# First stage of a fused attention kernel: both gate blocks side by side in eight PSUM banks, first loads one tile at a time

## The chip, the cores and the metric

One Trainium2 chip, one of its cores. The metric is the device time of one execution in microseconds, median of several runs. The kernel before took 1560.95 us (three runs, 1560.48 to 1561.99).

## What is computed

Four batches, 1024 rows of x (1024 wide) and 2048 rows of memory (512 wide) each:

```
memory_proj    = memory @ W_mem.T                    # W_mem is 1024 x 512
scores         = x @ memory_proj.T / sqrt(1024)
attn           = softmax(scores)
memory_context = attn @ memory_proj
gate           = sigmoid([x, memory_context] @ W_gate.T + b_gate) # W_gate is 1024 x 2048
out            = rmsnorm(x + gate * memory_context) * norm_w
```

The left half of W_gate (columns 0 to 1023) is applied to x, its right half to the memory context. The kernel doesn't form memory_proj. It multiplies x by W_mem first (q, 512 wide) and attends over the raw memory; and it multiplies the right half of W_gate by W_mem once (`wc`, 512 by 1024), to be applied to the attended raw memory at the end.

## The kernel before

All matmuls are 128x512 in fp32r. Every operand is held as a high part (an fp32r copy that ScalarE makes) and a low part (the difference, which VectorE makes, line 311), and every product is three matmuls (`PASSES`: high-high, high-low, low-high), 128 rows of depth at a time.

The program runs through stages. The first (up to the last matmul of line 1604 before line 1645) computes ten blocks of 512 columns: G0 and G1, the two halves of W_gate's right half, whose products with W_mem are `wc`; then X0 to X7, the 4096 rows of x, whose products are q. A block is 8 tiles of depth (t) by 4 tiles of columns of W_mem (c) by 3 passes: 96 matmuls. A block's four results stand in PSUM banks 0 to 3. ScalarE copies them out (`evacuate`), and they go to DRAM (`store_wc`, `store_q`). The later stages are the gate's part on x, the attention over 32 units of 128 rows, and the gate's part on the context with the norm.

On the way to a block each engine has a part of the work:

- SyncE issues all loads and stores of the stage, in one fixed order, and each waits for what it needs. The first loads come in three groups (`LEAD`: tiles 0-1, 2-3, 4-7), each first of W_mem and then of G0, four DMAs for each, one for each 32 partitions. After them come half blocks ("G1a", "X0b"; `load_half`, 1 MB each as four DMAs) into the two halves of the buffer `a_in`, in the order of the table `HALVES`. That table also holds "E0a" to "E1b", the left half of W_gate, which the next stage needs.
- VectorE transposes in blocks of 32 by 32: G0 tile by tile (128x512, line 259), all else by halves (128x2048, line 991), from `a_in` to `a_tf`. Then it makes the low parts.
- ScalarE makes the high parts, of W_mem (line 707), of G0's tiles (line 732) and of halves (line 711), and copies the banks out (lines 719 and 721).
- TensorE runs G0 tile by tile (`block_q0`), then nine blocks in a loop (`block_q`). A block needs its half (`xt_ready`) and its banks back (`q_ready`).

The transposed operand has one place, `a_xt`, 16 tiles in high and low. Half a of the next block may be split into it only when TensorE has passed the first half of the block before (`q_half`), and half b when it has finished that block (`q_done`). The results go out over the one buffer `prob`.

Of the kernel before, what the change touches and what calls it, by code (L numbers as in the profile page):

```python
# [20 lines left out]
def build(nc, x, mem, w_mem, w_gate, b_gate, norm_w, out):  # L21
# [28 lines left out]
    with ExitStack() as ctx:  # L50
# [37 lines left out]
        a_wc = prob[:].rearrange("p (c n) -> p c n", c=CT)  # L88
# [91 lines left out]
        def unit_tile(tile, u):  # L180
# [14 lines left out]
        w_loaded, g0_loaded = [sem(f"w_loaded{h}") for h in range(3)], [sem(f"g0_loaded{h}") for h in range(3)]  # L195
        w_hi, w_ready, g0_tile_t = sem("w_hi"), sem("w_ready"), sem("g0_tile_t")
        x0_tile_hi, x0_tile_ready = sem("x0_tile_hi"), sem("x0_tile_ready")
# [39 lines left out]
        HALVES = ("G1a", "G1b", "X0a", "X0b", "E0a", "X1a", "X1b", "E0b", "X2a", "X2b", "E1a", "X3a", "X3b", "E1b",  # L237
                  "X4a", "X4b", "X5a", "X5b", "X6a", "X6b", "X7a", "X7b")
# [23 lines left out]
        def tile_count(own, halves, t):  # L262

            return (halves, t // HT + 1) if t % HT == HT - 1 else (own, t - t // HT + 1)

        def tile_of_tf(t):
            return a_tf[:, BANK * t:BANK * (t + 1)]


        LEAD = ((0, 2), (2, 4), (4, 8))  # L270

        def lead_of(t):

            return t // 2 if t < HT else 2

        def w_piece(lead, n):

            lo, hi = LEAD[lead]
            src = a_wf.rearrange("p t (q c j) -> p t c q j", q=NQ, j=SQ)
            if lead == 2:  # L280
                ts, c = slice(lo, hi), n
                return (src[:, ts, c], *(a_w[:, part, ts, P * c:P * (c + 1)].rearrange("p t (q j) -> p t q j", q=NQ)
                                         for part in (HI, LO)))
            t, cs = lo + n // 2, range(2 * (n % 2), 2 * (n % 2) + 2)
            return (src[:, t, cs[0]:cs[1] + 1],
                    *(a_w[:, part, t, P * cs[0]:P * (cs[1] + 1)].rearrange("p (c q j) -> p c q j", q=NQ, j=SQ)
                      for part in (HI, LO)))

        def w_count(t, c):

            return 2 * t + c // 2 + 1 if t < HT else 2 * HT + c + 1
# [48 lines left out]
        def _(sp):  # L340
            for h, (lo, hi) in enumerate(LEAD):
                for q in range(NQ):
                    sp.dma_start(a_wf[SQ * q:SQ * (q + 1), lo:hi],
                                 w_mem[CHX * q + SQ * lo:CHX * q + SQ * hi, :].rearrange(
                                     "(t j) c -> j t c", j=SQ)).then_inc(w_loaded[h], 16)
                load_quadrants(sp, a_in, w_gate[0:BANK, D:2 * D], D, g0_loaded[h],
                               part=(lo // (hi - lo), DT // (hi - lo)))

            def load_half(name):
                n, k, h = nth(name) - 1, int(name[1]), "ab".index(name[2])  # L350
                if n < 2:
                    sp.wait_ge(g0_tile_t, HT * (n + 1))
# [4 lines left out]
                else:  # L357
                    src = w_gate[BANK * k:BANK * (k + 1), D * "EG".index(name[0]):D * "EG".index(name[0]) + D]
# [11 lines left out]
            def store_wc(k):  # L370
                sp.wait_ge(q_ready, CT * (k + 1))
                sp.dma_start(wc_dram[:, :, BANK * k:BANK * (k + 1)], a_wc).then_inc(block_stored, 16)
# [11 lines left out]
            load_half("X1b")  # L384
            load_half("E0b")
            store_wc(1)
            load_half("X2a")
            store_raw(1)
            load_half("X2b")
            load_half("E1a")  # L390
            store_q(0)
            load_half("X3a")
            load_half("X3b")
            load_half("E1b")
            store_q(1)
            load_half("X4a")
            load_half("X4b")
# [304 lines left out]
        def _(act):  # L702
            def split_w(lead):
                act.wait_ge(w_loaded[lead], 16 * NQ)
                for n in range(CT):
                    src, hi, _ = w_piece(lead, n)
                    nc.scalar.copy(hi, src).then_inc(w_hi, 1)  # L707

# [5 lines left out]
            def evacuate(k, c):  # L714
                if c == 0 and k > 0:
                    act.wait_ge(block_stored, 16 * k)
                act.wait_ge(q_done, k * CT + c + 1)
                if k < GB:
                    nc.scalar.copy(a_wc[:, c], bank[c][:]).then_inc(q_ready, 1)
# [7 lines left out]
            for t in range(DT):  # L727
                if t == LEAD[lead_of(t)][0]:
                    split_w(lead_of(t))
                act.wait_ge(g0_tile_t, t + 1)  # L730
                signal, _ = tile_count(x0_tile_hi, xt_hi, t)
                nc.scalar.copy(a_xt[:, HI, t, :], tile_of_tf(t)).then_inc(signal, 1)
            for k in range(LAST):
                following = BLOCKS[k + 1]
                act.wait_ge(half_t, nth(following + "a"))
                act.wait_ge(q_half, k + 1)
# [5 lines left out]
                if following == "X0":  # L742
                    act.wait_ge(half_t, nth("E0a"))
                    w7_split(A11, ef_x)
                if following == "X1":
                    act.wait_ge(half_t, nth("E0b"))
                    w7_split(A12, ef_y)
                if following == "X3":
# [21 lines left out]
            act.wait_ge(q_half, NBLOCKS)  # L770
# [210 lines left out]
        def _(dve):  # L981
            def split_w(lead):
                for n in range(CT):
                    dve.wait_ge(w_hi, lead * CT + n + 1)
                    src, hi, lo = w_piece(lead, n)
                    minus_hi(lo, src, hi).then_inc(w_ready, 1)

# [43 lines left out]

            for lead in range(len(LEAD)):
                split_w(lead)
                dve.wait_ge(g0_loaded[lead], 16 * NQ)
# [801 lines left out]
```

## Time and profile before

| | us |
|---|---|
| median of three runs | 1560.95 |
| the profiled execution's own time | 1556.9 |
| its span in the trace | 1555.1 |
| TensorE busy | 1528.3 (98%) |
| VectorE busy | 1080.3 (69%) |
| ScalarE busy | 549.0 (35%) |
| first matmul starts | 9.94 |
| last matmul of the first stage ends (first of line 1645 starts) | 231.60 |

The span is from the first to the last instruction. The profiled execution's own time is 1.8 us more than its span, and 4.05 us below the median of the runs without a profile. Start times below are counted from the start of the span. The record of a matmul runs until its modelled end, so that matmuls overlap: their starts say more than their busy time. A few matmul records are missing from the trace, so counts in a stretch are slightly low.

### The profile page before, as it was taken

Reading aid. Unit: us, or ns where it says so; the run is one execution under the profiler, and the core shown is the slowest. Engines: PE = TensorE matmul, PEld = TensorE weight load, DVE = VectorE, ACT = ScalarE, POOL = GpSimd, SP = SyncE. Lnnn points to the kernel's source line nnn. Section 1 sums busy time; section 2 is a strip of 40 time slices with the busy share of each in tenths; the row PEclk is TensorE's granted clock in tenths of the full one; section 3 lists DMA queues with packets and bytes.
Section 4 is the critical chain, followed back from the end, with each engine's and each line's share of the span. In section 5 each row is a group of like instructions: output and inputs, shape, how many; then the busy total and the mean of one; then the engine's idle time right before and its main releaser. Section 6 shows DMA issues by size and latency. Waiting matters only on the chain.

```text
span 1555.1 us, 21137 instructions
## 1 busy us (share of the span) xinstructions
PE 1528.3 (98%) x6720; PEld 1262.0 (81%) x6720; DVE 1080.3 (69%) x1502; ACT 549.0 (35%) x919; POOL 33.3 (2%) x72
## 2 busy tenths in 40 slices
PE   7999999999999999999999999999999999999997
PEld 5888888888888878888788888888888888888886
DVE  5654758777777864467446754567555899989987
ACT  4232342222222352244222432234222554444443
POOL 0000000000000000000000000000000001100011
PEclk9999999999999999999999999999999999999999
DMA  9997526333332786757584666757748645555553
GB/s 197 235 241 178 127 88 175 113 113 113 108 108 95 171 214 158 180 142 189 154 208 131 166 166 172 181 139 196 189 133 282 215 181 191 194 197 197 198 198 120
DMA packets 213399, 262.63 MB, mean 169 GB/s; under 512 B 19312, under 2 KB 136048, under 8 KB 213104
## 3 DMA queue, kind: packets, MB, share of 16 engines
q1 hardware_dynamic: 213360, 262.20, 59.8%
q8 instruction: 13, 0.21, 0.1%
q14 instruction: 26, 0.21, 0.1%
HBM read 170.39 MB, written 89.65 MB: 167 GB/s over the span
## 4 chain that ended last, share of the span: by engine, by line
PE 44%; DMA 3%; DVE 1%; issue 1%; ACT 1%; SPq 1%; POOL 0%; ACTq 0%; DVEq 0%; POOLq 0%
PE bank L1604 25%; PE bank L1753 19%; DMA prob_scratch<-prob 2%; DMA region_f<-in_ctx 1%; DMA region_f<-prob_scratch 1%; ACT prob L807 1%; DVE region_l L311 0%; SPq L453 0%; DVE region_n L311 0%; DVE max_part L1232 0%; DVE region_f L1328 0%; SPq L509 0%; ACT region_t L818 0%; ACT region_l L825 0%; POOL mean_sq L693 0%
## 5 line engine op out<-in xcount | busy, mean ns | idle before, releaser
L1604 PE MATMUL bank<-region_n,region_l 128*128 128x512 f32 x1536 | 353.6, 389 | 2.6 <-DVE region_l L311 2.6
L1604 PE MATMUL bank<-region_t,region_l 128*128 128x512 f32 x1536 | 353.7, 389 | 2.2 <-DVE region_l L311 2.1
L1604 PEld LDWEIGHTS bank<-region_t,region_l 128*128 128x128 f32 x1536 | 288.0, 188 | 63.8 <-issue 4.2
L1604 PEld LDWEIGHTS bank<-region_n,region_l 128*128 128x128 f32 x1536 | 288.2, 188 | 63.1 <-DVE region_l L311 2.9
L1604 PE MATMUL bank<-region_t,region_n 128*128 128x512 f32 x960 | 220.2, 392 | 11.6 <-DVE region_t L311 11.6
L1604 PEld LDWEIGHTS bank<-region_t,region_n 128*128 128x128 f32 x960 | 181.4, 189 | 49.9 <-DVE region_t L311 12.0
L825 ACT CAST region_l<-bank 128x512 fp32r<-128x512 f32 x128 | 75.0, 586 | 329.2 <-DVE bank L1261 329.0
L1261 DVE STREAM_TRANSPOSE bank<-region_f 128x512 f32<-128x512 f32 x128 | 88.7, 716 | 102.5 <-DMA region_f<-prob_scratch 100.3
L311 DVE TENSOR_TENSOR region_t<-region_f,region_t 128x1024 fp32r<-128x1024 f32 (+2 forms) x77 | 110.5, 1466 | 67.3 <-ACT region_t L711 60.5
L1645 PE MATMUL bank<-region_t,region_l 128*128 128x512 f32 x576 | 135.7, 389 | 0.0
L1645 PEld LDWEIGHTS bank<-region_t,region_l 128*128 128x128 f32 x576 | 108.1, 188 | 22.4
L1753 PE MATMUL bank<-region_t,region_l 128*128 128x512 f32 x480 | 120.6, 389 | 0.2 <-DVE region_l L311 0.2
L1753 PE MATMUL bank<-region_n,region_l 128*128 128x512 f32 x480 | 120.5, 389 | 0.0
L807 ACT ACTIVATE prob<-bank,neg_max 128x512 f32<-128x512 f32 x128 | 86.2, 686 | 84.0 <-DVE neg_max L1238 80.7
L1753 PEld LDWEIGHTS bank<-region_t,region_l 128*128 128x128 f32 x480 | 90.0, 188 | 19.3 <-issue 0.6
L1753 PEld LDWEIGHTS bank<-region_n,region_l 128*128 128x128 f32 x480 | 90.0, 188 | 19.1 <-DVE region_f L1328 0.4
L762 ACT CAST region_l<-region_f 128x512 fp32r<-128x512 f32 x80 | 49.5, 623 | 158.7 <-PE bank L1645 146.5
L1232 DVE TENSOR_REDUCE max_part<-bank 128x1 f32<-128x512 f32 x128 | 84.6, 663 | 17.7 <-PE bank L1604 17.6
L311 DVE TENSOR_TENSOR region_l<-bank,region_l 128x512 fp32r<-128x512 f32 x128 | 86.5, 676 | 8.5 <-ACT region_l L825 8.4
L1645 PE MATMUL bank<-region_n,region_l 128*128 128x512 f32 x384 | 92.2, 389 | 0.0
L311 DVE TENSOR_TENSOR region_n<-region_f,region_n 128x512 fp32r<-128x512 f32 (+3 forms) x70 | 78.6, 1140 | 15.8 <-ACT region_n L707 7.8
L1645 PEld LDWEIGHTS bank<-region_n,region_l 128*128 128x128 f32 x384 | 72.1, 188 | 15.0
(87 smaller groups left out, 1427.6 us busy)
## 6 DMA issues: line engine op xcount, KB each, us to landing
region_f<-in_ctx SPq DMA_DIRECT2D x128, 256.0 KB, 5.6
prob_scratch<-prob SPq DMA_DIRECT2D x128, 256.0 KB, 2.7
region_f<-prob_scratch SPq DMA_DIRECT2D x128, 256.0 KB, 4.3
region_f<-in_x SPq DMA_DIRECT2D x64, 256.0 KB, 6.1
region_f<-in_x SPq DMA_DIRECT2D x128, 128.0 KB, 2.7
region_f<-in_x SPq DMA_DIRECT2D x16, 1024.0 KB, 4.9
out<-region_f SPq DMA_DIRECT2D x31, 512.0 KB, 2.6
q_scratch<-prob SPq DMA_DIRECT2D x8, 1024.0 KB, 6.3
```

What stands on the lines that cost most here:

```text
L311: return nc.vector.tensor_tensor(dst, src, hi.bitcast(F32), ALU.subtract)
L762: nc.scalar.copy(z_x[i][:, HI], quarter(z_f[i])).then_inc(z_hi, 1)
L807: nc.scalar.activation(prob[:, BANK * j:BANK * (j + 1)], ps[j][:], ACT.Exp, bias=neg_max[:], scale=SCALE, accum_out=sum_part[:, j:j + 1]). ...
L825: nc.scalar.copy(b_pt[:, HI, TPB * g:TPB * (g + 1), :].rearrange("p k n -> p (k n)"), ps_t[g % 2][:]).then_inc(pt_hi, 1)
L1232: nc.vector.reduce_max(max_part[:, j:j + 1], ps[j][:], AX_X).then_inc(max_done, 1)
L1261: nc.vector.transpose(ps_t[g % 2][:].rearrange("p (k b i) -> p k b i", k=TPB, i=SQ), v[:, TPB * g:TPB * (g + 1)]).then_inc(pt_t, 1)
L1604: mm = nc.tensor.matmul(dst, lhs(a), rhs(b), start=first and n == 0, stop=last and n == len(PASSES) - 1)
L1645: mm = nc.tensor.matmul(ps[:], z_x[i][:, a, t, :], z_w[i][:, b, t, :], start=opens and t == 0 and n == 0, stop=closes and t == HT - 1 and ...
L1753: mm = nc.tensor.matmul(ps[:], x[:, a, P * t:P * (t + 1)], w[n][:, b, t, :], start=opens and t == 0 and m == 0, stop=closes and t == CH - ...
```

## The change

Four things, all in the first stage.

- G0 and G1 are computed side by side: G0 in banks 0 to 3, G1 in banks 4 to 7. TensorE takes two tiles of G0, two of G1, two of G0 and so on (`block_wc`). G1 has an operand place of its own (`a_xt1`, in a part of region_t that is not used in the stage), raw buffers of its own (`a_in1`, in prob and the second half of a_tf) and its own buffer for results (`a_wc[1]`, in the second half of the place of the raw W_mem).
- `LEAD` has five groups: tile 0, tile 1, then tiles 2-3, 4-5, 6-7. In each, G0 comes before W_mem. From the second group on, two tiles of G1 follow, those of the group before it: "one block later" is the place of G1's pair in the queue. All G1 loads come before the first half of x.
- G1 is transposed and split tile by tile like G0, not by halves. Both blocks' transposed tiles go through two slots each (`g_slot`).
- `HALVES` has no G1, and the halves of x stand one place further ahead of the stores: X1a before `store_wc(0)`, X2b before `store_raw(0)`, X3a before `store_q(0)`. The block X0 is written out before the loop, which now runs over seven blocks.

The number of matmuls, the bytes loaded and stored, and the later stages are as before.

SyncE, from its first instruction (line, destination<-source, shape of one DMA; W_mem and W_gate are the weights, x the input); before:

```order
L343 DMA region_f<-in_L_xattn_W_mem 32x2x512 x4
L252 DMA region_f<-in_L_xattn_W_gate 32x16x64 x4
L343 DMA region_f<-in_L_xattn_W_mem 32x2x512 x4
L252 DMA region_f<-in_L_xattn_W_gate 32x16x64 x4
L343 DMA region_f<-in_L_xattn_W_mem 32x4x512 x4
L252 DMA region_f<-in_L_xattn_W_gate 32x16x128 x4
L362 DMA region_f<-in_L_xattn_W_gate 32x16x128 x8
L362 DMA region_f<-in_x 32x16x128 x8
L362 DMA region_f<-in_L_xattn_W_gate 32x16x128 x4
L372 DMA wc_scratch<-prob 512x1x512
```

After, the same place:

```order
L257 DMA region_f<-in_L_xattn_W_gate 32x16x32 x4
L345 DMA region_f<-in_L_xattn_W_mem 32x512 x4
L257 DMA region_f<-in_L_xattn_W_gate 32x16x32 x4
L345 DMA region_f<-in_L_xattn_W_mem 32x512 x4
L352 DMA prob<-in_L_xattn_W_gate 32x16x64 x4
L257 DMA region_f<-in_L_xattn_W_gate 32x16x64 x4
L345 DMA region_f<-in_L_xattn_W_mem 32x2x512 x4
L352 DMA prob<-in_L_xattn_W_gate 32x16x64 x4
L257 DMA region_f<-in_L_xattn_W_gate 32x16x64 x4
L345 DMA region_f<-in_L_xattn_W_mem 32x2x512 x4
```

G0 of one tile moved to the head of the queue, in runs of 32 numbers (128 bytes); W_mem of one tile follows; line 352 is the first pair of G1's tiles, which used to come after all of G0, in the eight DMAs of line 362.

VectorE, from its first instruction (line 311 makes low parts: region_n is W_mem, region_t the gate blocks; line 259, after the change 1014, transposes a tile); before:

```order
L311 TENSOR_TENSOR region_n<-region_f,region_n 128x256 x4
L259 STREAM_TRANSPOSE region_f<-region_f 128x512 x2
L311 TENSOR_TENSOR region_t<-region_f,region_t 128x512 x2
L311 TENSOR_TENSOR region_n<-region_f,region_n 128x256 x4
L259 STREAM_TRANSPOSE region_f<-region_f 128x512 x2
L311 TENSOR_TENSOR region_t<-region_f,region_t 128x512 x2
L311 TENSOR_TENSOR region_n<-region_f,region_n 128x4x128 x4
```

After:

```order
L1014 STREAM_TRANSPOSE region_f<-region_f 128x512
L311 TENSOR_TENSOR region_t<-region_f,region_t 128x512
L311 TENSOR_TENSOR region_n<-region_f,region_n 128x256 x2
L1014 STREAM_TRANSPOSE region_f<-region_f 128x512
L311 TENSOR_TENSOR region_t<-region_f,region_t 128x512
L311 TENSOR_TENSOR region_n<-region_f,region_n 128x256 x2
L1014 STREAM_TRANSPOSE region_f<-prob 128x512 x2
L311 TENSOR_TENSOR region_t<-region_f,region_t 128x512 x2
L1014 STREAM_TRANSPOSE region_f<-region_f 128x512 x2
L311 TENSOR_TENSOR region_t<-region_f,region_t 128x512 x2
L311 TENSOR_TENSOR region_n<-region_f,region_n 128x256 x4
```

The gate tile now comes first and the low parts of W_mem last; a pair of G1's tiles stands between every two pairs of G0's.

VectorE where the gate blocks end and X0 begins, with the semaphores that each waits for (half_loaded0 and 1 are the landings of a half in either half of a_in; xt_hi is ScalarE's high part). Before, from G0's last tile on:

```order
L311 TENSOR_TENSOR region_t<-region_f,region_t 128x512 [waits xt_hi]
L991 STREAM_TRANSPOSE region_f<-region_f 128x2048 [waits half_loaded0,xt_ready]
L311 TENSOR_TENSOR region_t<-region_f,region_t 128x2048 [waits xt_hi]
L991 STREAM_TRANSPOSE region_f<-region_f 128x2048 [waits half_loaded1,xt_ready]
L991 STREAM_TRANSPOSE region_f<-region_f 128x2048 [waits half_loaded0,xt_ready]
L311 TENSOR_TENSOR region_t<-region_f,region_t 128x2048 [waits xt_hi]
```

After, from G1's last tiles on:

```order
L311 TENSOR_TENSOR region_t<-region_f,region_t 128x512 [waits g1_tile_hi] x2
L1025 STREAM_TRANSPOSE region_f<-region_f 128x2048 [waits half_loaded0,g1_tile_ready,g0_tile_ready]
L1025 STREAM_TRANSPOSE region_f<-region_f 128x2048 [waits half_loaded1]
L311 TENSOR_TENSOR region_t<-region_f,region_t 128x2048 [waits xt_hi]
```

The transposes of X0a and X0b now stand one behind the other, ahead of X0a's low part.

The diff, cut to its core:

```diff
+        a_xt1 = R1[:, 0:32 * KW].rearrange("p (h t n) -> p h t n", h=2, t=DT)
+        a_in1 = [v.rearrange("p (b t j) -> p b t j", t=DT // 2, j=SQ) for v in (prob[:], a_tf[:, 8 * KW:16 * KW])]
+        a_wc = [v.rearrange("p (c n) -> p c n", c=CT) for v in (prob[:], a_ef[:, 8 * KW:16 * KW])]
-        HALVES = ("G1a", "G1b", "X0a", "X0b", "E0a", "X1a", "X1b", "E0b", "X2a", "X2b", "E1a", "X3a", "X3b", "E1b",
-                  "X4a", "X4b", "X5a", "X5b", "X6a", "X6b", "X7a", "X7b")
+        HALVES = ("X0a", "X0b", "X1a", "X1b", "E0a", "X2a", "X2b", "E0b", "X3a", "X3b", "E1a", "X4a", "X4b", "E1b",
+                  "X5a", "X5b", "X6a", "X6b", "X7a", "X7b")
-        LEAD = ((0, 2), (2, 4), (4, 8))
+        LEAD = ((0, 1), (1, 2), (2, 4), (4, 6), (6, 8))
+        def g_slot(k, t):
+            n = 2 * k + t % 2
+            return a_tf[:, BANK * n:BANK * (n + 1)]
 (SyncE)
             for h, (lo, hi) in enumerate(LEAD):
+                load_quadrants(sp, a_in, w_gate[0:BANK, D:2 * D], D, g0_loaded[h],
+                               part=(lo // (hi - lo), DT // (hi - lo)))
                 ... (W_mem as before)
-                load_quadrants(sp, a_in, w_gate[0:BANK, D:2 * D], D, g0_loaded[h],
-                               part=(lo // (hi - lo), DT // (hi - lo)))
+                if h > 0:
+                    ... (four DMAs of G1's tiles 2h-2 and 2h-1)
 (SyncE, order of halves and stores)
-            for name in ("G1a", "G1b", "X0a", "X0b", "E0a"):
+            for name in ("X0a", "X0b", "X1a"):
                 load_half(name)
             store_wc(0)
-            load_half("X1a")
+            load_half("X1b")
+            store_wc(1)
+            for name in ("E0a", "X2a", "X2b"):
+                load_half(name)
             store_raw(0)
...
 (ScalarE)
+            for h, (lo, hi) in enumerate(LEAD):
+                for t in range(lo, hi):
+                    split_tile(0, t)
+                act.wait_ge(w_loaded[h], 16 * NQ)
+                for t in range(lo, hi):
+                    split_w(t)
+                if h > 0:
+                    for t in range(2 * h - 2, 2 * h):
+                        split_tile(1, t)
 (VectorE)
+            for h, (lo, hi) in enumerate(LEAD):
+                dve.wait_ge(g0_loaded[h], 16 * NQ)
+                for t in range(lo, hi):
+                    transpose_tile(0, t)
+                for t in range(lo, hi):
+                    split_tile(0, t)
+                for t in range(lo, hi):
+                    split_w(t)
+                if h > 0:
+                    dve.wait_ge(g1_loaded[h - 1], 16 * NQ)
+                    for t in range(2 * h - 2, 2 * h):
+                        transpose_tile(1, t)
+                    for t in range(2 * h - 2, 2 * h):
+                        split_tile(1, t)
 (TensorE)
+            def block_wc():
+                def tile(k, t):
+                    pe.wait_ge(g_tile_ready[k], t + 1)
+                    for c in range(CT):
+                        if k == 0:
+                            pe.wait_ge(w_ready, w_count(t, c))
+                        mm = product(bank[CT * k + c][:], lambda a: a_w[:, a, t, P * c:P * (c + 1)],
+                                     lambda b: (a_xt, a_xt1)[k][:, b, t, :], t == 0, t == DT - 1)
...
+                for pair in range(DT // 2):
+                    for k in range(GB):
+                        for t in range(2 * pair, 2 * pair + 2):
+                            tile(k, t)
-            block_q0()
-            with pe.Fori(1, NBLOCKS) as k:
-                block_q(k)
+            block_wc()
+            block_q(GB, 0)
+            with pe.Fori(GB + 1, NBLOCKS) as k:
+                block_q(k, (k - 1) * CT)
```

## Rows read from the trace of the kernel before

**Rows 1.** The page: span, and busy time of each engine.
```profile
span 1555.1 us, 21137 instructions
PE 1528.3 (98%) x6720; PEld 1262.0 (81%) x6720; DVE 1080.3 (69%) x1502; ACT 549.0 (35%) x919; POOL 33.3 (2%) x72
```

**Rows 2.** TensorE's waits, 0 to 210 us: total us, times, longest.
```profile
PE bank L1604 <- DVE region_t L311: 11.6, 2, 9.9
```

**Rows 3.** Windows: length, then busy time (count) by engine, TensorE clock, DMA.
```profile
9.94:13.94 4.00, 4.00 (x9) 3.14 (x10) 2.83 (x7) 1.42 (x5) 0.00 (x0) 1.00 1.13 223
13.94:22.66 8.72, 8.72 (x40) 7.18 (x38) 4.35 (x8) 3.30 (x6) 0.00 (x0) 1.00 1.19 214
22.66:24.70 2.04, 0.39 (x2) 0.00 (x0) 1.95 (x4) 1.21 (x2) 0.00 (x0) 1.00 1.22 218
24.70:231.60 206.90, 206.90 (x913) 171.29 (x913) 125.47 (x67) 71.16 (x70) 0.00 (x0) 1.00 0.77 176
```

**Rows 4.** Timeline, 0 to 40 us: start, length, engine, line, operation.
```profile
0.74 1.81 SPq L343 DMA_DIRECT2D region_f<-in_L_xattn_W_mem  x4
2.60 2.02 SPq L252 DMA_DIRECT2D region_f<-in_L_xattn_W_gate  x4
4.66 1.90 SPq L343 DMA_DIRECT2D region_f<-in_L_xattn_W_mem  x4
4.82 1.32 ACT L707 CAST region_n<-region_f 128x256 fp32r<-128x256 f32 x4 [2.80 <-DMA region_f<-in_L_xattn_W_mem]
5.26 1.43 DVE L311 TENSOR_TENSOR region_n<-region_f,region_n 128x256 fp32r<-128x256 f32 x4 [5.26 <-ACT region_n L707]
6.61 2.02 SPq L252 DMA_DIRECT2D region_f<-in_L_xattn_W_gate  x4
7.80 1.31 DVE L259 STREAM_TRANSPOSE region_f<-region_f 128x512 f32<-128x512 f32 x2 [1.11 <-DMA region_f<-in_L_xattn_W_gate]
8.55 1.21 ACT L732 CAST region_t<-region_f 128x512 fp32r<-128x512 f32 x2 [2.40 <-DVE region_f L259]
9.20 1.29 DVE L311 TENSOR_TENSOR region_t<-region_f,region_t 128x512 fp32r<-128x512 f32 x2
9.94 13.10 PE L1604 MATMUL bank<-region_t,region_n 128*128 128x512 f32 x48 [9.94 <-DVE region_t L311]
10.06 1.32 ACT L707 CAST region_n<-region_f 128x256 fp32r<-128x256 f32 x4 [0.30 <-DMA region_f<-in_L_xattn_W_mem]
13.09 1.31 DVE L259 STREAM_TRANSPOSE region_f<-region_f 128x512 f32<-128x512 f32 x2 [1.16 <-DMA region_f<-in_L_xattn_W_gate]
```

**Rows 5.** DMA, 2.6 to 22.6 us, then 4.8 to 7.0 us.
```profile
DMA packets 8289, 4.42 MB, mean 221 GB/s; under 512 B 4479, under 2 KB 7363, under 8 KB 8289
...
DMA packets 1439, 0.51 MB, mean 233 GB/s; under 512 B 1350, under 2 KB 1350, under 8 KB 1439
```

**Rows 6.** Timeline, 40 to 240 us.
```profile
56.85 2.31 DVE L991 STREAM_TRANSPOSE region_f<-region_f 128x2048 f32<-128x2048 f32 x1 [3.50 <-DMA region_f<-in_x]
68.65 1.91 ACT L711 CAST region_t<-region_f 128x2048 fp32r<-128x2048 f32 x1 [6.73 <-PE bank L1604]
70.59 4.49 DVE L311 TENSOR_TENSOR region_t<-region_f,region_t 128x2048 fp32r<-128x2048 f32 x2 [4.00 <-ACT region_t L711]
81.90 2.29 DVE L311 TENSOR_TENSOR region_t<-region_f,region_t 128x2048 fp32r<-128x2048 f32 x1 [2.40 <-ACT region_t L711]
88.37 2.31 DVE L991 STREAM_TRANSPOSE region_f<-region_f 128x2048 f32<-128x2048 f32 x1 [4.18 <-DMA region_f<-in_x]
90.41 1.91 ACT L711 CAST region_t<-region_f 128x2048 fp32r<-128x2048 f32 x1 [6.73 <-PE bank L1604]
231.60 5.60 PE L1645 MATMUL bank<-region_t,region_l 128*128 128x512 f32 x24
```

More of the change, by code:

```diff
@@ L193, in build @@
         const_ready = sem("const_ready")
[L195 to L197 removed]
+        w_loaded, g0_loaded = [sem(f"w_loaded{h}") for h in range(5)], [sem(f"g0_loaded{h}") for h in range(5)]
+        g1_loaded = [sem(f"g1_loaded{h}") for h in range(4)]
+        w_hi, w_ready = sem("w_hi"), sem("w_ready")
+        g_tile_t, g_tile_hi, g_tile_ready = ([sem(f"g{k}_tile_{what}") for k in range(2)]
+                                             for what in ("t", "hi", "ready"))
         half_loaded, half_t = [sem(f"half_loaded{s}") for s in range(2)], sem("half_t")
@@ L702, in _, with split_w, split_tile @@
         def _(act):
[L703 to L706, printed above, removed]
+            def split_w(t):
+                for n in range(2):
+                    src, hi, _ = w_piece(t, n)
                     nc.scalar.copy(hi, src).then_inc(w_hi, 1)
+            def split_tile(k, t):
+                act.wait_ge(g_tile_t[k], t + 1)
+                nc.scalar.copy((a_xt, a_xt1)[k][:, HI, t, :], g_slot(k, t)).then_inc(g_tile_hi[k], 1)
             def split_half(half):
@@ L725, in w7_split @@
                 nc.scalar.copy(z_w[i][:, HI], quarter(src)).then_inc(w7_hi, 1)
[L727 to L733, printed above, removed]
+            for h, (lo, hi) in enumerate(LEAD):
[7 more added lines that the diff above has]
+                        split_tile(1, t)
+            act.wait_ge(half_t, nth("X0a"))
+            act.wait_ge(q_half, 1)
+            split_half(0)
+            act.wait_ge(g_tile_t[1], HT)
+            for c in range(CT):
+                evacuate(0, c)
+            act.wait_ge(half_t, nth("X0b"))
+            split_half(1)
+            act.wait_ge(w_ready, 2 * DT)
+            for c in range(CT):
+                evacuate(1, c)
+            for k in range(GB, LAST):
                 following = BLOCKS[k + 1]
                 act.wait_ge(half_t, nth(following + "a"))
-                act.wait_ge(q_half, k + 1)
+                act.wait_ge(q_half, k)
                 split_half(0)
@@ L981, in _, with split_w, transpose_tile, split_tile @@
         def _(dve):
[L982 to L985, printed above, removed]
+            def split_w(t):
+                for n in range(2):
+                    dve.wait_ge(w_hi, 2 * t + n + 1)
+                    src, hi, lo = w_piece(t, n)
                     minus_hi(lo, src, hi).then_inc(w_ready, 1)
+            def transpose_tile(k, t):
+                if t >= 2:
+                    dve.wait_ge(g_tile_ready[k], t - 1)
+                nc.vector.transpose(g_slot(k, t).rearrange("p (b i) -> p b i", i=SQ), g_raw(k, t)
+                                    ).then_inc(g_tile_t[k], 1)
+            def split_tile(k, t):
+                dve.wait_ge(g_tile_hi[k], t + 1)
+                operand = (a_xt, a_xt1)[k]
+                minus_hi(operand[:, LO, t, :], g_slot(k, t), operand[:, HI, t, :]).then_inc(g_tile_ready[k], 1)
             def transpose_half(name, dst=a_tf):
@@ L1047, in _ @@
+            for k in range(2):
+                dve.wait_ge(g_tile_ready[k], DT)
+            transpose_half("X0a")
+            transpose_half("X0b")
+            split_half(1, 0)
             dve.wait_ge(xt_ready, 1)
-            transpose_half("G1a")
-            split_half(3, 0)
-            for k in range(LAST):
+            transpose_half("X1a")
+            split_half(2, 1)
+            for k in range(GB, LAST):
                 following = BLOCKS[k + 1]
-                dve.wait_ge(xt_ready, 2 * (k + 1))
+                dve.wait_ge(xt_ready, 2 * k - 2)
```

114 lines of the change are left out of this document (44 added, 70 removed).

## The prediction

> **What bounds the kernel now.** The page comes first: TensorE is busy for 1528.3 of 1555.1 us [rows 1]. So 26.8 us in all are open, and only what starts TensorE earlier or closes one of its gaps can count. The table of waits, cut to the first 210 us, names two waits, 11.6 us together, the longer 9.9 us [rows 2]: the start, and one more. The windows place them [rows 3]: the nine matmuls from 9.94 take 4.00 us; those from 13.94 run on; from 22.66 to 24.70 TensorE stands; from 24.70 to 231.60 it is busy all the time.
>
> The pace comes from the timeline. ScalarE's cast of half a waits for TensorE to pass the middle of a block, and two such casts start at 68.65 and 90.41 [rows 6]: 21.76 us for 96 matmuls, 0.2267 each. The stage has 960, so 217.6 us of work, and the next stage's first matmul starts at 231.60 [rows 6]. What isn't work is 14.0 us: 9.94 ahead of the first matmul; 1.96 as the first nine take 4.00 in place of 2.04; 1.81 in the gap (2.04 less one matmul); 0.3 left over. The trace gives the granted clock as 1.00 there too, but the spacing of 0.44 us against 0.2267 is that of the lower of the clock's two levels, 1.2 against 2.4 GHz, after TensorE had done nothing.
>
> Why it starts at 9.94 stands in the timeline [rows 4]: SyncE needs 1.8 to 2.0 us to issue four DMAs, W_mem of two tiles comes first, G0's two tiles after it, landed at 7.80, and transpose, cast and low part of a tile take 2.14 us more. Why it stands at 22.66: a block needs 1 MB of W_mem and G0 for 24 matmuls (5.4 us at pace), and the DMA engines bring 221 GB/s [rows 5], 4.7 us for 1 MB; with the latencies on top G0 eats nearly as fast as it is fed.
>
> **The start.** All is counted from the span's start. Four DMAs of the G form are issued in 2.02 us, every 0.53 us, and four of the W form in 1.85, groups following at 0.05 [rows 4]. So after the change G0's tile 0 is issued from 0.74 to 2.8, W_mem's tile 0 to 4.7, G0's tile 1 to 6.7, W_mem's tile 1 to 8.6, and G1's first pair to 10.7.
>
> W_mem's first group landed at 4.82, 2.27 us after its issue ended at 2.55 [rows 4]; a tile of half the size lands about as soon, so W_mem tile 0 at 6.9. By then G0's tile 0 (landed near 5.3) has been transposed and cast. From W_mem's landing to its first low part it is 0.44 us to VectorE's start and 0.42 for the operation (4.82, 5.26, then 1.43 us for four that overlap slightly) [rows 4], so TensorE starts at 6.9 + 0.9 = 7.8. The bounds: 7.3, if the smaller DMAs are issued and land faster; 8.8, if G0's tile 0 lands 3.2 us after its issue, as G0's first group did (4.62 to 7.80), and its steps push those of W_mem back.
>
> Tile 0 is 12 matmuls, at the slow spacing for 4.0 us: done at 7.8 + 2.72 + 1.96 = 12.5. Tile 1 is ready at 8.6 + 2.3 + 0.9 = 11.8, so the slow stretch covers it. It ends at 15.2.
>
> Then G1's tile 0. Its loads are issued from 8.7 on, in the very form (128 KB each) of G0's first group, which went from first issue at 2.60 to landing at 7.80, 5.2 us, with the DMA engines already at 223 to 233 GB/s [rows 3, 5]; 1.05 MB had to be in by then. After the change it is 1.57 MB by 13.9; at 221 GB/s from 2.6 that is there at 9.7, so it is issue and latency that count, and I take 4.8: landed at 13.5. With 2.14 for transpose, cast and low part [rows 4] it is ready at 15.7: a gap of 0.5.
>
> **After that** TensorE has more to do for each byte. Two tiles of both blocks are 48 matmuls, 10.9 us, for 1.57 MB, 7.1 us of DMA, where G0 alone had 5.4 us for 1.05 MB. VectorE's part for them is four transposes (0.66 each), four low parts (0.65) and four of W_mem (0.36): 6.7 us by the merged rows [rows 4]. So both run ahead. The tightest is G0's tile 2, wanted at 15.7 + 5.4 = 21.1: VectorE is done with G1's first pair at 16.3 and needs 3.0 for the next two tiles of G0 and their first piece of W_mem, which 2.62 MB at 221 GB/s bring by 14.5 and the issue by 17: ready at 19.6 to 20. The gap of 1.81 and the 0.3 go.
>
> Non-work after the change: 7.8 + 1.96 + 0.5 = 10.3, where it was 14.0. Gain 3.7 us, bounds 3.0 (G1's first pair takes all of 5.2 us, start of matmuls no matter, and 0.3 left over) and 4.4 (pair landed before 13, tile 1's end at 15.0 decides).
>
> **What is moved otherwise costs nothing, and this is why.** TensorE wants X0a at 10.3 + 43.5 = 53.8 and X0b at 64.7. All gate and weight loads are 6.29 MB, X0 2.1 MB more: 8.39 MB at 214 to 221 GB/s from 2.6 is 41 to 42; X0b's issue also waits for G0's tile 7 to be transposed, near 32. VectorE transposes X0a and X0b one behind the other, so X0a's low part waits for X0b's landing: say 44, then 2.31 and 2.29 [rows 6]: 48.6, 5.2 us to spare. Behind it are queued only the transpose of X1a and X0b's low part, which ScalarE's cast after the copies of banks 0 to 3 (from 48.4, G0 being done 5.4 us before G1) sets at 54, wanted at 64.7. X0 finds banks 0 to 3 free at 49.5. In the SyncE queue `store_wc(0)` waits until then and X1b's load stands behind it; it lands near 57, wanted at VectorE for a split after 76. Later blocks have the cover of before: the cast of half a starts at 68.65 and its low part is done at 72.9, where the block ends at 79.5; the half that VectorE had to wait for at 88.37 (4.18 us) cost TensorE nothing [rows 3, 6]. The other edits of SyncE's order move landings by a few us within some 6 us of cover. Should that cover be gone, each us late is a us lost. The later stages see the same, earlier by the gain.
>
> **The narrow loads.** Tiles 0 and 1 of G0 go in runs of 128 bytes, 4096 packets, which the trace doesn't show. Next to it stand 256-byte packets: 1350 of 1439 in a stretch that moved 233 GB/s, no slower than the mixed 221 [rows 5]. I take 1.5 times the time per byte (1.8 us for a tile, not 1.2), which is under the 2.0 us of issuing it; a cost below nothing is excluded, since the issue sets it. Even at double the time the 1.57 MB are in at 9.7 + 2.4 = 12.1, before the 13.5.
> The Trainium skill, page "DMA: Bandwidth & Descriptors", section Specifications, says that transfers under 512 bytes fall from line rate because the engine then reads, modifies and writes. By that rule the 256-byte stretch should have been slower than the rest, and the trace doesn't bear it out; if it held only for the 128-byte runs, the second rival below would be the result.
>
> **Rivals.**
> 1. The slow stretch lasts longer or the pair lands later: TensorE starts earlier but with fewer tiles behind it. Were the slow stretch 8 us, not 4, tile 1 would end at 7.8 + 5.4 + 3.9 = 17.1 and the gain be 14.0 − 11.7 = 2.3. The same if issue is slower beside 128-byte runs, G1's tile landing at 15. For it: only one start is in the trace. Against it: the load on TensorE over its first 4 us is the same. Gain 1 to 2.9, middle 2.2: 1558.8.
> 2. 128-byte runs cost four times per byte: 2 tiles x 3.6 us = 7.2 more, 1.57 MB in at 17, G1's tile at 17.2 + 2.1 = 19.3, non-work 13.9, gain 0.1: 1560.9. For it nothing in rows, against it the 233 GB/s.
> 3. Slower: TensorE waits for X0. Place: VectorE's transpose of X0b, ahead of X0a's low part. It decides once X0b lands after 49.2, and makes the kernel slower than before from 52.9 on. If the load were issued only after G1's last tile (38) and took 10 us with others in flight, it would be 48; a start of X0 at 59 gives 1562.5. Against it: the queue is never more than 2 MB deep there, 9.5 us.
>
> **How the numbers follow.** The sum is against the profiled execution: 1556.9 − 3.7 = 1553.2. The median of the runs is 4.05 above its time, and I carry that: 1560.95 − 3.7 = 1557.25. The forecast gets 0.68 (gain 2.9 to 4.4, its own range 1556.5 to 1558.1), rival 1 0.16, rival 2 0.07, rival 3 and whatever else costs more than the gain 0.09. A measurement of this kernel tells 0.2%, 3.1 us, from no change: that cuts the forecast's lower end, so faster is 0.60, same 0.31 (0.08 of the forecast, rivals 1 and 2), slower 0.09. The range goes from 1556.0 to 1560.9.
>
> **What would show it.** Right: first matmul at 7.3 to 8.8; about ten matmuls at the slow spacing; one gap under 1 us near 15, ended by VectorE's low part of a G1 tile; none after; line 1689 starting at 227.9. Wrong: a gap near 12 (narrow runs or issue), a gap near 21 (VectorE), any gap near 54 (X0), slow spacing beyond 12.5, or a stage end later than 228.7.

## The result, and the profile after

The changed kernel takes 1555.75 us (median of 12 runs, 1553.76 to 1558.44), the kernel before 1559.02 us (12 runs, 1557.29 to 1561.99). The ratio is 0.9981, 95% interval 0.9974 to 0.9989: 3.0 us faster, between 1.7 and 4.1. The forecast was 3.7 us faster. The profiled execution took 1554.77 us, with a span of 1553.0 where it was 1555.1 [rows 1].

The page, and TensorE's waits in the first 210 us (us in total, times, longest), which answer to [rows 1, 2]:

```profile
span 1553.0 us, 21179 instructions
PE 1530.3 (99%) x6720; PEld 1263.6 (81%) x6720; DVE 1082.0 (70%) x1518; ACT 550.2 (35%) x929; POOL 33.3 (2%) x72
...
PE bank L1642 <- DVE region_n L311: 7.2, 1, 7.2
PE bank L1642 <- DVE region_t L311: 0.2, 1, 0.2
```

Of the 11.6 us of waits 7.4 are left. Both traces hold all 6720 matmuls, 960 of them in the stage, so that no record is missing and the counts in a stretch can be trusted. The timeline of the start, against [rows 4]:

```profile
0.74 2.00 SPq L257 DMA_DIRECT2D region_f<-in_L_xattn_W_gate  x4
2.78 1.88 SPq L345 DMA_DIRECT2D region_f<-in_L_xattn_W_mem  x4
4.64 0.71 DVE L1014 STREAM_TRANSPOSE region_f<-region_f 128x512 f32<-128x512 f32 x1 [4.64 <-DMA region_f<-in_L_xattn_W_gate]
...
6.21 0.71 ACT L712 CAST region_n<-region_f 128x256 fp32r<-128x256 f32 x2 [0.20 <-DMA region_f<-in_L_xattn_W_mem]
6.64 0.76 DVE L311 TENSOR_TENSOR region_n<-region_f,region_n 128x256 fp32r<-128x256 f32 x2
...
7.22 8.01 PE L1642 MATMUL bank<-region_t,region_n 128*128 128x512 f32 x24 [7.22 <-DVE region_n L311]
8.68 2.02 SPq L352 DMA_DIRECT2D prob<-in_L_xattn_W_gate  x4
...
13.28 1.31 DVE L1014 STREAM_TRANSPOSE region_f<-prob 128x512 f32<-128x512 f32 x2 [1.83 <-DMA prob<-in_L_xattn_W_gate]
14.02 1.22 ACT L716 CAST region_t<-region_f 128x512 fp32r<-128x512 f32 x2 [3.21 <-DVE region_f L1014]
14.68 1.29 DVE L311 TENSOR_TENSOR region_t<-region_f,region_t 128x512 fp32r<-128x512 f32 x2
...
15.42 24.78 PE L1642 MATMUL bank<-region_t,region_n 128*128 128x512 f32 x108 [0.20 <-DVE region_t L311]
```

G0's tile has landed at 4.64 and W_mem's at 6.21; the first matmul starts at 7.22. SyncE issues G1's first pair from 8.68; it lands at 13.28, and 2.14 us later TensorE goes on. By the records, which run to a matmul's modelled end, the gap is 0.20 us; by the starts, which the prediction counted with, it is 0.35. From there TensorE doesn't stand still in the stage. Later in the same timeline:

```profile
45.59 2.31 DVE L1025 STREAM_TRANSPOSE region_f<-region_f 128x2048 f32<-128x2048 f32 x1 [2.00 <-DMA region_f<-in_x]
47.83 2.25 DVE L311 TENSOR_TENSOR region_t<-region_f,region_t 128x2048 fp32r<-128x2048 f32 x1
...
60.50 2.31 DVE L1025 STREAM_TRANSPOSE region_f<-region_f 128x2048 f32<-128x2048 f32 x1 [5.46 <-DMA region_f<-in_x]
...
227.72 4.47 PE L1689 MATMUL bank<-region_t,region_l 128*128 128x512 f32 x19
```

The stage ends at 227.72, where it was 231.60 [rows 6]: 3.88 us of gain. But the last matmul of the program starts only 2.13 us sooner (1542.40 against 1544.53). 1.75 us were lost on the way, and TensorE's windows show where: the wait between the attention of the first two units, 2.75 us from start to start in the changed kernel and 2.83 in the kernel before, and what follows (length, busy (count), granted clock, DMA share, GB/s). Before:

```profile
579.00:582.40 3.40, 0.95 (x6) 1.00 0.41 147
582.40:585.80 3.40, 3.40 (x15) 1.00 0.03 11
```

After:

```profile
575.70:578.40 2.70, 0.34 (x2) 1.00 0.26 99
578.40:582.20 3.80, 3.79 (x10) 0.55 0.12 23
582.20:589.80 7.60, 7.60 (x35) 1.00 0.68 195
```

Behind that wait the granted clock is 0.55 over 3.8 us, which is the lower level, 1.2 GHz, for nearly all of them: 10 matmuls where about 17 fit at 0.2267 us each. The 48 matmuls of that unit take 12.63 us, not 11.01. In this execution the kernel before kept its clock there. Whether that belongs to the change is left to the experiments.

### The profile page after: what moved, and what is told of

It reads as the page before. It is cut to its first block, busy times and chain, and to the rows that moved or that the text cites. A ratio compares the mean times of both kernels' runs of the same rounds, so it can differ in the third digit from the quotient of the medians.

```text
span 1553.0 us, 21179 instructions
## 1 busy us (share of the span) xinstructions
PE 1530.3 (99%) x6720; PEld 1263.6 (81%) x6720; DVE 1082.0 (70%) x1518; ACT 550.2 (35%) x929; POOL 33.3 (2%) x72
## 4 chain that ended last, share of the span: by engine, by line
PE 88%; DMA 5%; SPq 2%; DVE 2%; issue 1%; ACT 1%; POOL 0%; ACTq 0%; DVEq 0%; POOLq 0%
PE bank L1642 49%; PE bank L1689 20%; PE bank L1797 19%; DMA prob_scratch<-prob 3%; DMA region_f<-in_ctx 1%; SPq L257 1%; DMA am_out<-q_scratch 1%; DMA region_f<-prob_scratch 0%; DVE region_l L311 0%; SPq L459 0%; ACT prob L830 0%; DVE region_n L311 0%; DVE max_part L1270 0%; SPq L345 0%; SPq L475 0%
## 5 line engine op out<-in xcount | busy, mean ns | idle before, releaser
L1642 PE MATMUL bank<-region_t,region_n 128*128 128x512 f32 x960 | 220.5, 392 | 7.4 <-DVE region_n L311 7.2
```

Of the source, the lines that this page charges most:

```text
L1642: mm = nc.tensor.matmul(dst, lhs(a), rhs(b), start=first and n == 0, stop=last and n == len(PASSES) - 1)
```

## Experiments

Two theories stood. One: the gain is made of an earlier start and of a feed (issue, DMA, VectorE) that the second block's matmuls cover, and what is given back later is chance. The rival: the start is all, the eight banks add nothing, and the loss behind 576 us belongs to the change.

All were timed in turn with the kernel before on their chip. The times (ratio to before with interval), the first real matmul, the end of the stage, the wait near 580 us (start to start of the matmuls around it), and the 48 matmuls behind it, all from each one's profile:

| | ratio | first | stage end | wait | 48 matmuls |
|---|---|---|---|---|---|
| before | | 9.94 | 231.60 | 2.83 | 11.01 |
| before again | 0.9999 (0.9990 to 1.0009) | 9.85 | 231.36 | 3.17 | 12.62 |
| changed | 0.9981 (0.9974 to 0.9989) | 7.22 | 227.72 | 2.75 | 12.63 |
| changed again | 0.9975 (0.9965 to 0.9985) | 7.18 | 228.10 | 4.06 | 12.38 |
| new start alone | 1.0016 (1.0007 to 1.0025) | 7.32 | 235.12 | 2.45 | 11.01 |
| groups of two tiles | 0.9989 (0.9980 to 0.9999) | 8.74 | 229.56 | 3.00 | 12.62 |
| W_mem first | 0.9991 (0.9982 to 1.0000) | 9.07 | 228.37 | 4.65 | 13.33 |
| stores first | 0.9977 (0.9965 to 0.9988) | 7.69 | 228.18 | 3.75 | 13.65 |
| warm | 0.9979 (0.9970 to 0.9989) | 7.27 | 228.13 | 3.81 | 12.53 |
| fill | 0.9969 (0.9958 to 0.9981) | 7.35 | 227.76 | 3.05 | 11.01 |
| warm and fill | 0.9980 (0.9971 to 0.9989) | 7.30 | 228.21 | 2.85 | 11.05 |
| ScalarE issues | 0.9975 (0.9966 to 0.9984) | 8.02 | 228.49 | 3.19 | 12.64 |
| all three | 0.9963 (0.9949 to 0.9976) | 8.32 | 226.04 | 3.59 | 11.01 |
| X0b late | 1.0019 (1.0008 to 1.0029) | 7.22 | 233.63 | 3.74 | 13.81 |

**The new start without the eight banks.** The kernel before, with these edits alone:

```diff
-        LEAD = ((0, 2), (2, 4), (4, 8))
+        LEAD = ((0, 1), (1, 2), (2, 4), (4, 6), (6, 8))
 (SyncE, each group) G0's DMAs ahead of W_mem's
 (VectorE, ScalarE)  G0's tile first, then W_mem's two pieces
```

> The kernel before with only the new start: five groups, G0 ahead of W_mem, one tile at a time at first; G0 still runs alone in banks 0 to 3 and G1 comes by halves after it. Theory (the start gives the 2.7 us, the second block beside the first closes the gaps that this opens): first matmul at 7.2, but a gap of about 1 us before G0's tile 2 and one of 1 to 2 us before G1's first half, so the next stage starts at 229 to 230 (before 231.60, changed kernel 227.72). Rival (the gain is all in the start, the eight banks add nothing): no gap over 0.4 us and the stage ends at 227.7 to 228.2.

Its TensorE timeline:

```profile
7.32 7.33 PE L1590 MATMUL bank<-region_t,region_n 128*128 128x512 f32 x24 [7.32 <-DVE region_n L301]
16.37 16.57 PE L1590 MATMUL bank<-region_t,region_n 128*128 128x512 f32 x72 [1.73 <-DVE region_n L301]
37.53 52.68 PE L1590 MATMUL bank<-region_t,region_n 128*128 128x512 f32 x224 [4.58 <-DVE region_t L301]
```

The start is as early as in the changed kernel, and the kernel is slower than before. Both gaps that the theory named are there, and larger: 1.7 us before tile 2 and 4.6 us before G1's first half, as G0 is done at 32.8 but G1a has only landed at 30.8 and its transpose, cast and low part take until 37.4. The clock then stood at its lower level for 3.4 us from 38.0. The rival falls: the early start alone is worth nothing. The theory's sizes were too small, 229 to 230 against 235.12.

What closes the first gap is the work on G1 between G0's tiles: in the changed kernel G0's tile 1 is done at 15.1 and W_mem's piece for tile 2 at 19.0, so that without it TensorE would wait there as well. The second gap also hangs on something else. In this run G1 still comes by halves, 1 MB at a time, and in the changed kernel tile by tile. No run keeps G0 and G1 one behind the other with G1 in tiles, so how much of the 4.6 us each of the two takes away is not shown.

**Which load, in which piece.** Two edits of the changed kernel's `LEAD` loop:

```diff
-        LEAD = ((0, 1), (1, 2), (2, 4), (4, 6), (6, 8))
+        LEAD = ((0, 2), (2, 4), (4, 6), (6, 8))         # groups of two tiles
```

> The changed kernel with its first loads in groups of two tiles (no run under 256 bytes), all else as changed. Theory (issue and latency set the start, single tiles make it earlier, but G1's first pair decides): first matmul at 8.0 to 8.4, tile 1 of G0 done at about 16, the next stage starts at 228.2 to 228.5, 0.5 to 0.8 us later than in the changed kernel. Rival (128-byte runs cost much, and what single tiles gain they lose): the stage ends at 227.7 or earlier.

G1's first pair then stands behind two groups of two tiles, 2.1 MB in place of 1.05, in as many DMAs.

```diff
 (SyncE, each group)                                     # W_mem first
-    G0's four DMAs, then W_mem's
+    W_mem's four DMAs, then G0's
```

> The changed kernel with W_mem issued ahead of G0 in each group, as before. Theory (the last to land starts the first matmul, and G0's tile has 2.1 us of work behind it where W_mem has 0.9): first matmul at 8.8, stage end 1.2 us later than changed, at 228.9. Rival (both have to land anyway): first matmul within 0.3 of 7.2.

Groups of two start at 8.74 and end the stage 1.5 to 1.8 us later than the changed kernel; 0.5 to 0.8 was expected. The first 12 starts were at the slow spacing, and G1's pair landed late:

```profile
15.08 1.30 DVE L1014 STREAM_TRANSPOSE region_f<-prob 128x512 f32<-128x512 f32 x2 [0.64 <-DMA prob<-in_L_xattn_W_gate]
```

It was issued at 8.72, as in the changed kernel, and came at 15.08, not 13.28: twice the bytes lay ahead of it, which I hadn't counted. So this run doesn't weigh the 128-byte runs by themselves; it shows only that the start with single tiles is the better one as a whole. W_mem first starts at 9.07, 1.85 us later, as its last tile to land has the long chain behind it; the stage ends only 0.3 to 0.65 us later than in the two profiles of the changed kernel, because only six starts were at the slow spacing and nothing was left to wait for at G1's first pair. Both theories hold in sign; in size the first was 1 us too small and the second 0.6 to 0.9 too large.

**Stores first.** SyncE's order back:

```diff
-            for name in ("X0a", "X0b", "X1a"): load_half(name)
-            store_wc(0)
-            load_half("X1b")
+            for name in ("X0a", "X0b"): load_half(name)
+            store_wc(0)
+            load_half("X1a")
+            load_half("X1b")
+            ... (store_raw(0), store_q(0), store_raw(1), store_q(1) likewise ahead of a half)
```

> The changed kernel with the stores back ahead of the halves of x in SyncE's order (store_wc(0) before X1a, store_raw(0) before X2b, store_q(0) before X3a, store_raw(1) before E1a, store_q(1) before X4a). Theory (all of it lies in cover): X1a lands some 6 us later, TensorE has no gap, stage end 227.7 as changed, time the same within 0.1%. Rival (the order is needed once both blocks run side by side): a gap at X1, near 75 us, of 1 us or more.

X1a was transposed at 60.29 and not at 50.55, 9.7 us later and not 6, and TensorE has no gap there. From its first matmul to the end of the stage it takes 220.5 us, as the changed kernel does. This part of the change is worth nothing here.

**X0b late.** Is the cover at X0 real, and what does it cost when it is gone?

```diff
+            sp.wait_ge(q_done, 1)
             load_half("X0b")
```

> The changed kernel with X0b's load held back until G0's first bank is done (about 46 us); X1a follows it. X0b then lands near 53 in place of 45.6. Theory (VectorE transposes X0b ahead of X0a's low part, and the cover is 3.5 us in the changed kernel's trace): X0a's low part is done at 57.5, TensorE waits 3.5 to 4.5 us at 53.6, and the stage ends that much later, at 231.5 to 232.2. Rival (X0a doesn't hang on X0b): no gap over 0.5 us.

```profile
53.26 2.31 DVE L1027 STREAM_TRANSPOSE region_f<-region_f 128x2048 f32<-128x2048 f32 x1 [10.28 <-DMA region_f<-in_x]
55.50 2.25 DVE L311 TENSOR_TENSOR region_t<-region_f,region_t 128x2048 fp32r<-128x2048 f32 x1
...
57.80 8.49 PE L1644 MATMUL bank<-region_t,region_n 128*128 128x512 f32 x29 [3.89 <-DVE region_t L311]
```

X0b 7.7 us late gives a wait of 3.9 us, so the cover was about 3.7; in the changed kernel's own trace X0a's low part is done at 50.08 and X0's first matmul starts at 53.64, which is 3.6. The rest of the 5.5 to 5.9 us by which the stage ends later is mostly the clock, at its lower level for 3.4 us from 58.8 on (about 1.7 us). The forecast of 231.5 to 232.2 left that out; the stage ended at 233.63. The rival falls, and one load that comes 7.7 us late makes the changed kernel slower than before, 1.0019.

**The slow first matmuls, and the issue.** The edits are cut to their core. Warm puts 16 bf16 matmuls on a constant ahead of the first real one; ScalarE issues takes eight DMAs from SyncE; all three is both with the fill below:

```diff
+            for _ in range(16):                                     # warm, on TensorE
+                nc.tensor.matmul(bank[7][:], w[:, 0:P], w[:, 0:BANK], start=True, stop=True)
```

```diff
+            for h in range(2):                                      # on ScalarE, in place of SyncE
+                for q in range(NQ):
+                    act.dma_start(a_wf[SQ * q:SQ * (q + 1), h:h + 1], ...).then_inc(w_loaded[h], 16)
```

> The changed kernel with 16 extra bf16 matmuls of 128x512 on a constant, on TensorE ahead of its first real one (bank 7, which G1 overwrites later). Theory (the slow spacing of the first ten matmuls is the low clock of an engine that did nothing before, and costs about 2.3 us in the changed kernel): they use up the slow stretch from about 1.5 us on, the first real matmuls run at 0.227, tile 0 and 1 are eaten sooner and G1's first pair decides: its tile 0 starts at 15.4 as before, so the gap there grows to some 2.5 us and the stage ends only 0.2 to 0.4 us sooner, at 227.4. Rival (the slow stretch is what the stage loses): the stage ends 2.3 us sooner, at 225.4.

> The changed kernel with the loads of W_mem's tiles 0 and 1 (eight DMAs) issued by ScalarE in place of SyncE, at the same time as SyncE issues G0's. Theory (G1's first pair decides when the stage runs on, and SyncE's issue, 0.5 us a DMA, decides when the pair lands; but the slow first matmuls hide most of that): the pair is issued from 4.7 in place of 8.7 and lands at 9.5 to 10, first matmul at 7.2 to 7.7 (ScalarE's table load comes later), no gap at 15; the slow stretch of 2 us and more now counts, and the stage ends at 227.0 to 227.5, 0.2 to 0.7 us sooner than changed. Rival (the DMA engines, not the issue, set the landing): the pair lands at 12.5 or later and the stage ends as changed, at 227.7 or later.

> The changed kernel with all three: W_mem's first tiles issued by ScalarE, 16 extra matmuls at the start, 10 at the wait near 576 us. Theory (each of the two start limits hides the other, so only both together pay): the stage ends at 225.0 to 225.6, 2.1 to 2.7 us sooner than changed, the clock holds after 576, and the time is 3 to 4.5 us below the changed kernel's, about 0.995 to 0.996 of before. Rival (the two are not tied): the stage ends at 227.4, as the sum of the single effects (-0.3 and +0.4) says, and the time is that of e6, 0.997.

Warm, TensorE's timeline:

```profile
7.27 2.98 PE L1644 MATMUL bank<-region_t,region_n 128*128 128x512 f32 x12
11.19 3.01 PE L1644 MATMUL bank<-region_t,region_n 128*128 128x512 f32 x12 [0.93 <-DVE region_n L312]
15.83 74.42 PE L1644 MATMUL bank<-region_t,region_n 128*128 128x512 f32 x327 [1.64 <-DVE region_t L312]
```

The first tile of G0 takes 2.98 us, not some 5, and all of the gain turns into waits of 0.93 and 1.64 us: G1's tile comes at 15.83. The stage ends at 228.13, no sooner, where 227.4 was forecast. The low clock at the start costs the changed kernel nothing; G1's first pair sets the pace.

With ScalarE issuing:

```profile
4.91 1.28 ACT L716 ACT_TABLE_LOAD   x1 [4.91 <-issue]
5.41 0.71 DVE L1019 STREAM_TRANSPOSE region_f<-region_f 128x512 f32<-128x512 f32 x1 [5.41 <-DMA region_f<-in_L_xattn_W_gate]
...
10.80 1.29 DVE L1019 STREAM_TRANSPOSE region_f<-prob 128x512 f32<-128x512 f32 x2
```

The pair was there when VectorE came to it at 10.80 (13.28 in the changed kernel), so issue and not the DMA engines set its landing. But G0's tile 0, now beside W_mem's on the DMA engines, landed at 5.41, not 4.64, and the first matmul came at 8.02. ScalarE's table load, now behind its DMAs, is over at 6.19 and the tile's transpose at 6.12, so it cost under 0.1. The slow matmuls, 12 of them here, are uncovered, and the stage ends at 228.49. That is a miss by 1 us, on the side of the rival's number but not by its mechanism. All three:

```profile
8.32 15.92 PE L1649 MATMUL bank<-region_t,region_n 128*128 128x512 f32 x69 [1.59 <-DVE region_n L312]
8.43 0.70 DVE L1020 STREAM_TRANSPOSE region_f<-region_f 128x512 f32<-128x512 f32 x1
...
11.10 1.30 DVE L1020 STREAM_TRANSPOSE region_f<-prob 128x512 f32<-128x512 f32 x2
```

TensorE starts at 8.32, later than in the changed kernel, and runs without a gap to the end of the stage at 226.04, 1.7 to 2.1 us sooner. Each limit hid the other, as the theory said; the stage ended 0.4 us later than forecast, and the start came later than in the changed kernel. It is the fastest version tried, 0.9963 of before, 5.8 us; its interval overlaps with the changed kernel's. Against the changed kernel on the same chip it is 1.7 us faster by the medians, where 3 to 4.5 were forecast. That is what the stage gave; of the rest, which was to come from the fill, nothing shows.

**The fall of the clock near 580 us.** Ten extra matmuls in the wait:

```diff
             with_memory(0, 0)
+            for _ in range(10):
+                nc.tensor.matmul(ps_am1[:], b_mt[:, 0, HI, 0, 0:P], b_mt[:, 0, HI, 0, :], start=True, stop=True)
             with_memory(1, ps=ps_am1)
```

> The changed kernel with 10 extra matmuls (results thrown away, bank 7) between the attention of unit 0 and that of unit 1, where TensorE waits for 2.5 us and more near 576 us. Theory (the gain of the stage is partly given back there, as the clock falls to its lower level for 3.4 us after that wait): the extra matmuls, 2.3 us, fit into the wait, the granted clock stays at 1.0 there, and the time is 1.2 to 1.7 us below the changed kernel's, near 0.9970 of before. Rival (the give-back is just the exchange with DRAM taking longer): clock or not, the unit's matmuls start no earlier and the time stays at 0.998.

> Both together. Theory: the two savings add, 0.3 us of the first and 1.2 to 1.7 us of the second; 0.9965 to 0.9970 of before. Rival: no better than the changed kernel, 0.998.

Fill, then before again, in TensorE's windows:

```profile
575.70:578.40 2.70, 2.65 (x12) 1.00 0.37 140
578.40:582.20 3.80, 3.45 (x15) 1.00 0.09 11
```

```profile
580.00:582.00 2.00, 0.00 (x0) 1.00 0.18 69
582.00:586.00 4.00, 3.54 (x10) 0.64 0.05 12
```

> The changed kernel once more, beside the other two on the same chip. Theory: stage end at 227.7 to 228.2 (landings vary by 0.5 us), one wait of 2.5 to 4.5 us near 576 with the clock at its lower level behind it, and 0.998 of before. Rival (the fall of the clock in its first profile was chance): the granted clock stays at 1.0 after the wait.

> The kernel before once more, as a run of its own, unchanged. Theory (the wait near 580 us is in both kernels alike, and whether the clock falls behind it hangs on when it comes and how long it is, not on the change): stage end within 0.5 us of 231.6; the clock may fall behind the wait, which is then 2.5 to 4.5 us long; ratio to before 1.000 within 0.001. Rival (only the changed kernel loses its clock there, and that gives back 1.7 us of its gain in every run): the granted clock stays at 1.0 behind the wait.

The kernel before, run again, loses its clock there too: 0.64 over 4 us, and 12.62 us for the 48 matmuls. Of the eleven profiles without the fill nine have the fall (all but the first of before and the new start alone); of the three with it none. So the wait and the fall behind it are in both kernels. That the changed one isn't hit more often is shown by the mean granted clock over the span, which is on record for each execution and from which a fall of 3.4 us takes 0.0011: it is 0.9971 in 105 executions of the kernel before, 0.9969 in 21 of the changed one, with a standard error of 0.0002, and 0.9977 in the 23 with the fill. The 1.75 us between the first two profiles was chance.

That the fill keeps the clock is shown. That it saves time is not: 0.9969 against 0.9981 and 0.9975 without it, intervals overlapping, and warm and fill is at 0.9980, the rival's number, where warm alone is at 0.9979. The traces say the same. From the last matmul ahead of the wait to the last one of the program it is 967.5 to 968.1 us in the three profiles with the fill, 966.8 to 968.5 in the six where the clock fell for 3.4 us, 969.4 to 970.6 in the three where it fell for 6.8, and 965.0 and 967.3 in the two where it held by itself. So what the fill gives behind the wait is lost again later. The rival of that run, that the exchange with DRAM sets the time, is not excluded.

## Why the prediction was right

It was right in direction and size, and its mechanism held. Two terms of the sum were off with opposite signs, and that they cancelled is luck. Counted by starts, what isn't work is now 7.22 + 2.40 + 0.47 = 10.1 us, where 10.3 was forecast: the start, what the slow spacing costs, and the gap at G1's first pair with the one late start behind it.

- The start: 7.8 forecast, 7.22 measured, just outside the bound of 7.3. W_mem's tile landed 1.55 us after its issue ended, not 2.27; I had taken the delay of a group twice the size.
- The slow stretch: the first 12 matmuls were to take 4.68 us (2.72 and 1.96 of loss) and took 5.12, with ten spacings of 0.43. The two errors cancel: tile 1 of G0 left TensorE free at 15.07 where 15.2 was forecast, and at 15.46 in the second profile.
- G1's first pair: landing 13.5 forecast, 13.28 measured; ready 15.7 against 15.42; gap 0.5 against 0.35. This was the term that decides, as the warm run shows.
- Afterwards no gap: right. G0's tile 2 was wanted at 20.9, and the first piece of W_mem for it was done at 19.0.
- The end of the stage: 227.9 forecast, 227.72 and 228.10 in the two profiles. Before, it was 231.60 and 231.36, so the stage gave 3.3 to 3.9 us, and the ratios say 3.0 and 3.9 (0.9981 and 0.9975). The times alone, 1.7 to 4.1 us, would not tell the forecast from rival 1; the stage end does, which under rival 1 would have been 229.3. From the end of the stage to the last matmul ahead of the wait near 576 us it is 347.9 us in every profile but one (348.0), whatever the start; the spread of the time comes from behind it.
- The absolute time: 1557.25 forecast, 1555.75 measured, just under the lower end of the range, 1556.0. The median of 1560.95 that it was counted from came from three runs, and twelve gave 1559.02, so the 4.05 us carried from the profiled execution to the median were 2.1 in truth (1.0 in the changed kernel). Only the difference from before was forecast rightly.
- The cover at X0: 5.2 us forecast, 3.6 to 3.7 measured. VectorE was done with G1 at 38.8 (38 forecast), X0b was there at 45.59 (44 forecast). "Each us late is a us lost" was too mild: 3.9 us of wait cost 5.5 or more, as the clock fell behind it. Rival 3 would have been worse than priced.
- X1b was transposed at 60.50, 3.5 us later than thought, in cover all the same. The other order of stores is worth nothing, as forecast.
- The narrow runs: 1.5 times the time per byte was taken. In the trace the 4096 packets of 128 bytes took a median of 13 ns; those of 256 bytes took 18 in the trace of before and 21 in that of the changed kernel, so 1.2 to 1.4 times per byte. Rival 2's four times didn't come: the pair landed at 13.28, not at 17. The Trainium skill, page "DMA: Bandwidth & Descriptors", section Specifications, puts the smallest transfer for full rate at 512 bytes. The trace doesn't show its step there: in the first 60 us of both kernels a packet of 512 bytes took a median of 44 ns, no less per byte than one of 256, and over the whole trace one of 1 KB took 46 ns. How busy the DMA engines were differs between these groups, so they are no clean comparison.
- Rival 1 (a longer slow stretch costs its length) was partly wrong as an argument. The slow stretch was longer, and it cost nothing, since the pair came later still. The run with the stretch taken away shows the same.

What the prediction missed: it gave no thought to clock falls behind later waits, which cost single executions 1.4 to 2.8 us over the 48 matmuls behind the wait. That is the main reason why the profiled difference is 2.1 us where the ratio gives 3.0.

## What to carry to other kernels

When a stage is starved at its start, ask how much work each loaded byte carries. Starting earlier with the same work per byte only moved the wait, and made the kernel slower. Two blocks side by side on one shared operand, the second loaded in tiles too, closed it; how much side by side and how much tiles did was not separated. Before removing a limit, look for the one just behind it: the low clock and the issue queue each hid the other, and removing either alone was worth nothing. One profile of each kernel is a poor measure of a small gain. With two of each here, the difference of the spans is 0.3 to 4.0 us, depending on the pair. So compare stage ends, and look at the granted clock behind waits of some 2.5 us and more. That a clock fall is avoided doesn't yet mean that time is saved.

## What the runs showed of the hardware

Near 576 us TensorE waits 2.45 to 4.65 us (start to start) in the eleven profiles without the fill. In nine of them the granted clock fell to the lower level, for 3.4 us in six and for 6.8 in three; after waits of 2.45 and 2.83 it held. It fell after one of 2.75, so the length alone doesn't decide. Two longer waits in the first stage, 4.97 us with the new start alone and 4.28 with X0b late, had a fall behind them too. In four of the nine the clock fell when TensorE was running again, 0.4 to 1.0 us after the wait; in the other five it had fallen 0.2 to 1.9 us before TensorE went on.

The count of first matmuls at the slow spacing of 0.43 us differs between executions of one kernel: 8 and 6 before, 10 and 12 after the change, and 6 to 12 over all kernels without the warm matmuls. Landings of the first loads varied too: with the same order of the first loads the first matmul came at 7.18 to 7.69 us, and G1's first pair landed at 13.28 and 13.66 in the two profiles of the changed kernel.
